# VectorE's order at the block changes of a two-branch MLP kernel: two low parts of x ahead of the fourth gating product, one weight's low part behind the first

## What is computed

```python
xn = layernorm(x)
s  = silu(xn @ Wg_a.T)
s  = zero_smallest_half_by_abs(s) * (xn @ Wu_a.T)
a  = s @ Wd_a.T
b  = (silu(xn @ Wg_b.T) * (xn @ Wu_b.T)) @ Wd_b.T
out = x + a * silu(b)
```

## Time and profile before

| | |
|---|---|
| median of 3 runs | 2782.82 us (2781.74 to 2786.43) |
| profiled execution | 2784.59 us, span of the trace 2782.8 us |
| PE matmul | 2753.9 us busy, 99% of the span |
| DVE | 2307.4 us, 83% |
| ACT | 1352.7 us, 49% |
| POOL | 388.3 us, 14% |
| granted PE clock, mean | 0.996 |

### The profile page before, as it was taken

How to read it: one execution, slowest core, us unless ns; L and a number is a source line. 1 busy time by engine, 2 the same in 40 slices (tenths; PEclk the granted TensorE clock), 3 DMA queues, 4 the chain that set the end, 5 groups by cost and what they waited for, 6 DMA issues and landing times. The chain is left out here.

```text
span 2782.8 us, 31374 instructions
## 1 busy us (share of the span) xinstructions
PE 2753.9 (99%) x12204; PEld 2281.1 (82%) x12204; DVE 2307.4 (83%) x3002; ACT 1352.7 (49%) x1386; POOL 388.3 (14%) x161
## 2 busy tenths in 40 slices
PE   9999999999999999999999999999999999999999
PEld 7778888878788888888878888888887888888887
DVE  7676999999967698998986678999897767999971
ACT  4234998332444477631144557671115446776110
POOL 5565443044400000000020000000011000000000
PEclk9999999999999999999999999999999999999999
DMA  6898888579766555556656655555666664555564
GB/s 235 308 328 286 293 288 280 211 251 357 255 193 196 181 188 192 189 203 219 249 190 195 192 180 190 195 196 194 240 223 195 193 196 173 195 196 193 189 233 170
DMA packets 135097, 614.28 MB, mean 221 GB/s; under 512 B 12752, under 2 KB 12752, under 8 KB 89168
## 3 DMA queue, kind: packets, MB, share of 16 engines
q1 hardware_dynamic: 134992, 612.94, 63.2%
HBM read 492.31 MB, written 120.59 MB: 220 GB/s over the span
## 5 line engine op out<-in xcount | busy, mean ns | idle before, releaser
L632 PE MATMUL ps<-w_split,hid_ring 128*128 128x512 f32 x4096 | 935.2, 390 | 6.8 <-ACT hid_buf L1136 4.6
L632 PEld LDWEIGHTS ps<-w_split,hid_ring 128*128 128x128 f32 x4096 | 769.4, 188 | 171.5 <-issue 7.9
L1380 DVE TENSOR_SCALAR_CACHE_REDUCE ranks<-key_buf,cand 128x2752 int16<-128x2752 f32 x248 | 762.9, 3076 | 5.8
L961 ACT ACTIVATE signs_row<-key_buf,cand 128x2752 bf16<-128x2752 f32 x248 | 642.6, 2591 | 191.6 <-DVE cand L1389 182.0
L877 PE MATMUL ps<-xnT,w_split 128*128 128x512 f32 x1376 | 535.3, 389 | 0.0
L876 PE MATMUL ps<-xnT,w_split 128*128 128x512 f32 x1376 | 535.3, 389 | 0.0
L875 PE MATMUL ps<-xnT,w_split 128*128 128x512 f32 x1376 | 535.3, 389 | 0.0
L1206 POOL TENSOR_TENSOR w_split<-w_raw,w_split 128x1024 fp32r<-128x1024 f32 (+2 forms) x118 | 290.2, 2467 | 377.3 <-ACT w_split L928 137.0
L875 PEld LDWEIGHTS ps<-xnT,w_split 128*128 128x128 f32 x1376 | 258.3, 188 | 53.7
L876 PEld LDWEIGHTS ps<-xnT,w_split 128*128 128x128 f32 x1376 | 258.3, 188 | 53.6
L877 PEld LDWEIGHTS ps<-xnT,w_split 128*128 128x128 f32 x1376 | 258.3, 188 | 53.3
(11 more groups left out here) (146 smaller groups left out, 2907.0 us busy)
## 6 DMA issues: line engine op xcount, KB each, us to landing
w_split<-split SPq DMA_DIRECT2D x272, 1024.0 KB, 4.8
split<-w_split SPq DMA_DIRECT2D x72, 1024.0 KB, 6.8
w_raw<-w_a SPq DMA_DIRECT2D x100, 512.0 KB, 4.2
w_raw<-t_dram SPq DMA_DIRECT2D x78, 512.0 KB, 3.3
w_raw<-w_b SPq DMA_DIRECT2D x42, 512.0 KB, 4.9
w_extra_raw<-t_dram SPq DMA_DIRECT2D x42, 512.0 KB, 3.6
t_dram<-t_buf SPq DMA_DIRECT2D x20, 1024.0 KB, 8.6
w_extra_raw<-w_a SPq DMA_DIRECT2D x30, 512.0 KB, 3.6
```

Of the source, the lines that this page charges most:

```text
L632: ins = pe.matmul(ps[:, 2 * t + half, :], h, w[:, half * TB:(half + 1) * TB], start=(first and n == 0), stop=last and stop)
L961: act.activation(signs_row[:, :], keys[:, t, :], ACT.Sign, bias=cand_f[:, t:t + 1], scale=-1.0, accum_out=counts[:, t:t + 1]).then_inc(act ...
L1380: dve.tensor_scalar(ranks[:, :], keys[:, t, :], cand_f[:, t:t + 1], 0.0, ALU.is_lt, ALU.add, accum_out=counts[:, t:t + 1]).then_inc(sel_st ...
```

## The change

It edits only DVE's queue. At each of the three block changes, low parts 6 and 7 of the next block's x, which stood behind gate 3 (at the head of the next block's `run`), now stand ahead of it. The low part of weight tile 2, which stood ahead of gate 0, now stands behind it. The last block's end is not touched.

```diff
                 if b > 0:
-                    for n in (6, 7):
-                        xn_low(b, n)
                     last_outputs(b - 1, OUT_POOL)
...
                 if not last_block:
                     for n in range(NJ - 1 - AHEAD - X_PARTS_AT, 6):
                         xn_low(b + 1, n)
-                    w_lows(b + 1, 0, 3)
+                    w_lows(b + 1, 0, 2)
                 for t in range(NT - 1 if last_block else NT):
+                    if not last_block and t == 1:
+                        w_lows(b + 1, 2, 3)
+                    if not last_block and t == NT - 1:
+                        for n in (6, 7):
+                            xn_low(b + 1, n)
                     if t < NT - 1:
                         dve.wait_ge(ad_mm, b * (NT - 1) + (t + 1))
```

## The result

The changed kernel takes 2787.88 us (median of 17 runs, 2782.38 to 2791.96) against 2782.54 us before (17 runs beside them): ratio 1.0018, 95% interval 1.0011 to 1.0026. It is slower by some 5 us; the forecast was 2779.3 us. The profiled execution took 2789.89 us, span 2788.1 us. Every step of the forecast up to PE's tile 3 came as worked out; the one behind it, that `s_lo(1)` would come earlier, did not.

A forecast was written before the change was run, and what follows sets the result against it. PE, busy 99% of the span, was taken to bound the kernel, waiting for DVE's low parts of x at block changes. Gains of 2.0 + 1.6 + 1.7 = 5.3 us off 2784.59 gave 2779.3 us, range 2776 to 2786.

The forecast's parts named there:

- Gates, tile 2's low part, POOL's first addition held, low part 6 first by 0.03 us: Into block 3, low part 6 starts at 2100.02, ahead of POOL's second addition at 2100.05, and takes 0.69 us.
- first rival: At low part 6, POOL's second addition goes first and holds it until about 2102.99; 2785.9 us, slower; chance 0.28.
- Tile 1 and tile 3: Into block 3, PE starts tile 1 at 2100.85 and tile 3 at 2108.10; 1.34 us won are left there.
- `s_lo(1)` done by 2116.2: Into block 3, tile 8's load goes 2.5 us earlier, so tile 6 starts at 2116.30, 2.0 us won.
- third rival: Ahead of tile 6, tile 8's load lands no earlier and `s_lo(1)` stays where it was; 2784.6 us; chance 0.07.
- The clock stays high: Into block 3, no clock fall after tile 1's 0.6 us gap: tile 1 takes 2.73 us, saving 1.69.
- second rival: The new gap ahead of tile 3 drops the clock, 1.7 us each; 2784.4 us at all three changes; chance 0.15.
- The sum: Over the three block changes, 2.0 + 1.6 + 1.7 = 5.3 us won, 3.5 us less than the median.

The follow-up runs named there:

- stores_late: Changed kernel with the stores of the third and fourth token tile's result moved behind the load of weight tile 8: 2776.84 us, ratio 0.9980 to the kernel before.
- after_s_early: Changed kernel with `s_lo(1)` ahead of weight tile 8's low part instead of behind it: 2776.39 us, ratio 0.9985 to the kernel before.
- w_only: Kernel before with only weight tile 2's low part moved behind gate 0, x's low parts staying behind gate 3: 2784.58 us, ratio 1.0010.
- before_s_early: Kernel before with `s_lo(1)` ahead of weight tile 8's low part: 2777.32 us, ratio 0.9984.
- x_only: Against the kernel before, only low parts 6 and 7 of x moved ahead of gate 3: 2785.09 us, ratio 1.0008.
- w3_early: Changed kernel with weight tile 3's low part ahead of the addition to gate 3: 2784.13 us, ratio 1.0005 to the kernel before.

## Why the prediction was wrong

**Gates, tile 2's low part, POOL's first addition held, low part 6 first by 0.03 us:** right at all three changes (by 0.05 to 0.06 us in the records). Low part 6 took 0.68 us, and the first rival (POOL first) did not happen.

**Tile 1 and tile 3:** right, to 0.06 us at block 3: a gap of 0.61 us (0.6 forecast) and a new one of 1.47 (1.6). The 1.3 us won at tile 3 were there, 1.4 by the records.

**`s_lo(1)` done by 2116.2:** this is the step that failed. I took the load of tile 8 to go about 2.5 us earlier, which it nearly did (2.2), and to land as much earlier, which it did not (2114.56 against 2114.61 at block 3, and 0.5 to 0.6 us later at the other two): I carried over the landing time of a trace in which it was issued alone, 2.4 us behind its neighbours. The edit had moved the third store 1.4 us later, through POOL's additions, and tile 7's and 8's loads earlier, and I counted these moves as free, each by its own deadline and not by what they do to tile 8's load. That was my third rival, at 0.07. `stores_late` shows the cause: the same VectorE order with the bunch broken up is some 10 us faster. `after_s_early` shows the same from the other side: with `s_lo(1)` taken out from behind that load, and the bunch left as it is, it is 9 us or more faster.

**The clock stays high:** wrong too, and a consequence. At block 3 the 1.4 us won at tile 3 and the 0.54 us wait that was there before came together ahead of tile 6 as one gap of 1.87 us (1.94 and 2.00 at the others), and the clock fell behind that. Over all runs the mean granted clock is nearly the same before (0.9976, 33 runs of it beside the first experiments) and after (0.9974). So the changed kernel doesn't lose by more falls; it loses because the fall before lay inside the time that PE would have waited for `s_lo(1)` anyway, at least in part, and now lies behind it. The traces have three falls at the changes, but 0.9974 over a run is 7.2 us lost, of which the trace has some 3.4 in block 0 (0.50 from 610.7 to 617.4); so a run of either kernel has nearer two there, by this estimate. The second rival had a fall in the gap ahead of tile 3; none was seen there.

**The sum:** I had 5.3 us won, 3.5 against the median. At tile 6 nothing of it was left (20.82 to 20.87 us from the down product's end at block 3, 20.42 to 21.05 at block 2, 22.31 to 22.90 at block 1), and 1.7 us of low clock were added behind it at each: 0.05 + 0.63 + 0.59 + 3 x 1.7 = 6.4 us, against 6.15 measured there. My bound for the third rival, the time of before, left out that second half.

## What to carry to other kernels

A wait removed is only a gain up to the next one that doesn't move: follow the chain to the first step whose release comes from something else (here a load), and ask of that step what the earlier traffic will do to it. Transfers have to be counted together; a landing time read in a trace holds for the spacing of issues in that trace. And place matters for the clock: no gap up to 1.5 us at these changes was followed by a fall, so several small gaps were cheaper here than their sum in one place. A fall ahead of a wait that stays cost less (1.1 us in `w_only`) than one behind it (1.7).

## What the runs showed of the hardware

Between VectorE's operations with two SBUF inputs and GpSimd's additions, a few hundredths of a microsecond decide who goes first. Low part 6, whose record starts 0.04 to 0.07 us before that of POOL's second addition, took 0.68 us at all 15 changes of the five traces with that order; in the earlier trace rows POOL is first by 0.02 us, and VectorE's operation takes 2.92 us. The Trainium skill (SBUF — State Buffer, "Who interferes with whom") says that whichever issues first keeps the other out for a whole instruction; the trace agrees (3.27 us for POOL's first addition behind tile 2's low part, 2.42 without).

The length of PE's gap alone doesn't decide whether the clock falls behind it. At the changes into blocks 2 and 3 it fell behind 4 of 6 gaps of 2.06 or 2.07 us (not in `before_s_early`), behind one of two of 2.87 us (`w_only`), behind all four of 1.84 to 2.09 us of the changed kernel's two traces, behind one of 2.50 us but not one of 1.94 (`x_only`), not behind one of 2.73 us in `w3_early`, and never behind one of 1.5 us or less. A 512 KB load took 4.1, 4.9, 7.1 or 7.4 us to land, by what was issued around it.
